# Gated cross attention and a grouped feed forward block on one core: the sums of token blocks are made ahead and kept in memory

## The reference

```python
x = x + jnp.tanh(g_xattn[0]) * xattn(_layernorm(x), ctx_2048, ctx_2048, wq, wk, wv, wo)
x = x + jnp.tanh(g_ffn[0]) * ffn(_layernorm(x), gate_w, mask_up_w, gate_proj_w, up_proj_w, down_proj_w, inv_map)

def xattn(x, k_cache, v_cache, wq, wk, wv, wo):
    q, k_new, v_new = (einsum('bsd,ed->bse', x, w) for w in (wq, wk, wv))
    k, v = concatenate([k_cache, k_new], 1), concatenate([v_cache, v_new], 1)
    attn = softmax(einsum('bqd,bkd->bqk', q, k) / sqrt(512))
    return einsum('bqd,ed->bqe', einsum('bqk,bkd->bqd', attn, v), wo)

def ffn(h, ...):
    scores = softmax(x @ gate_w.T)                       # 64 experts, the best 8 are kept as w_e
    flat = w_e[:, inv_map]                               # 8 groups of 8
    scalar = flat.sum(-1)
    soft = softmax(where(flat == 0, -1e9, flat))
    xg = x[:, None, :] + einsum('ngi,ghi->ngh', soft, mask_up_w)
    g, u = einsum('ngh,gih->ngi', xg, gate_proj_w), einsum('ngh,gih->ngi', xg, up_proj_w)
    return einsum('ng,ngh->nh', scalar, einsum('ngi,ghi->ngh', silu(g) * u, down_proj_w))
```

## Time and profile before

| | us |
|---|---|
| time before, three runs | 1113.67, 1112.12, 1113.27 (median 1113.27) |
| the profiled execution: its own time | 1115.06 |
| its span in the trace | 1113.3 |
| PE busy | 1061.3 (95%) |
| attention, until PE's last probability transposes (about) | 306 |
| quads 0 to 2, until product_1 of quad 3 | 404 |
| product_1 of quad 22, second pass | 732 |
| mean granted clock | 0.977 of full speed |

### The profile page before, as it was taken

The page is one execution under the profiler, slowest core; times in us unless marked ns, Lnnn a source line. Parts: engine busy times, 40 slices in busy tenths (PEclk is TensorE's granted clock), DMA queues, the critical chain, the costliest instruction groups (busy, mean ns, idle before and its releaser), DMA issues.

```text
span 1113.3 us, 14594 instructions
## 1 busy us (share of the span) xinstructions
PE 1061.3 (95%) x5388; PEld 903.4 (81%) x5388; DVE 754.8 (68%) x1328; ACT 378.4 (34%) x635; POOL 604.1 (54%) x479
## 2 busy tenths in 40 slices
PE   8999999999976779999999999979999999999997
PEld 7988998998865667887888888858888888888885
DVE  7775666666579648787787876776656665666554
ACT  5333333332332323433334332333233333332331
POOL 1212201210344656766687668767777777777751
PEclk9999999999988889999999999989999999999998
DMA  9112223323683411122212211472322112221202
GB/s 331 58 39 95 63 64 83 79 81 48 124 264 102 89 46 64 34 81 46 72 60 48 71 64 62 138 231 86 105 72 71 62 36 72 72 71 47 70 26 76
DMA packets 86861, 94.75 MB, mean 85 GB/s; under 512 B 20240, under 2 KB 71184, under 8 KB 86800
## 3 DMA queue, kind: packets, MB, share of 16 engines
q1 hardware_dynamic: 86432, 93.80, 28.8%
q10 hardware_dynamic: 368, 0.15, 0.0%
HBM read 70.67 MB, written 23.27 MB: 84 GB/s over the span
## 4 chain that ended last, share of the span: by engine, by line
PE 86%; DVE 7%; DMA 2%; issue 2%; POOL 1%; ACT 1%; SPq 1%; POOLq 0%; DVEq 0%; ACTq 0%
PE bank L67 42%; PE bank L1500 35%; PE bank L1506 3%; PE bank L1514 2%; PE bank L1331 1%; DMA x_raw<-x 1%; DMA soft_stacks<-soft_out 1%; DMA w_raw<-in_w_qkvo 1%; PE bank L1383 1%; DVE seed L906 0%; PE bank L1402 0%; POOL wd_lo L573 0%; SPq L426 0%; DVE soft L1026 0%; POOL wgu_lo L565 0%
## 5 line engine op out<-in xcount | busy, mean ns | idle before, releaser
L565 POOL TENSOR_TENSOR wgu_lo<-wgu_raw,wgu_hi 128x768 fp32r<-128x768 f32 (+1 forms) x132 | 214.6, 1633 | 97.7 <-ACT wgu_hi L756 95.5
L1500 PE MATMUL bank<-x2t_hi,wgu_lo 128*128 128x512 f32 x616 | 244.4, 397 | 17.8 <-ACT tmp L819 5.2
L1500 PE MATMUL bank<-x2t_lo,wgu_hi 128*128 128x512 f32 x616 | 242.5, 394 | 0.0
L1500 PE MATMUL bank<-x2t_hi,wgu_hi 128*128 128x512 f32 x616 | 242.1, 393 | 0.0
L756 ACT CAST wgu_hi<-wgu_raw 128x768 fp32r<-128x768 f32 (+1 forms) x132 | 95.7, 727 | 240.6 <-PE bank L1506 194.8
L1217 DVE TENSOR_TENSOR xres<-xres,bank 128x512 f32<-128x512 f32 x176 | 119.9, 682 | 63.2 <-PE bank L67 63.2
L1500 PEld LDWEIGHTS bank<-x2t_hi,wgu_lo 128*128 128x128 f32 x616 | 117.4, 191 | 44.7 <-issue 17.8
L67 PE MATMUL bank<-wd_hi,at_second 128*128 128x512 f32 x352 | 138.7, 394 | 0.0
L1500 PEld LDWEIGHTS bank<-x2t_hi,wgu_hi 128*128 128x128 f32 x616 | 117.2, 190 | 24.9
L1500 PEld LDWEIGHTS bank<-x2t_lo,wgu_hi 128*128 128x128 f32 x616 | 117.5, 191 | 23.4
L67 PE MATMUL bank<-wd_hi,at_first 128*128 128x512 f32 x264 | 105.4, 399 | 14.2 <-issue 13.0
(11 more groups left out here) (194 smaller groups left out, 2275.8 us busy)
## 6 DMA issues: line engine op xcount, KB each, us to landing
wgu_raw<-in_w_gate_up SPq DMA_DIRECT2D x44, 512.0 KB, 3.9
wd_raw<-in_w_down SPq DMA_DIRECT2D x22, 512.0 KB, 4.9
a_stacks<-a_stack SPq DMA_DIRECT2D x22, 192.0 KB, 1.8
a_stack<-a_stacks SPq DMA_DIRECT2D x22, 192.0 KB, 3.8
ctxt_raw<-in_ctx_t SPq DMA_DIRECT2D x8, 512.0 KB, 11.6
ctx_raw<-in_ctx SPq DMA_DIRECT2D x8, 512.0 KB, 9.3
x<-x_raw SPq DMA_DIRECT2D x8, 512.0 KB, 4.0
w_raw<-in_w_qkvo SPq DMA_DIRECT2D x6, 512.0 KB, 7.8
```

The source lines that it names most:

```text
L565: nc.gpsimd.tensor_tensor(wgu_lo[:, group], wgu_raw[quad.set][:, group], f32(wgu_hi[:, group]), ALU.subtract).then_inc(s_fw_lo, 1)
L1500: last = nc.tensor.matmul(out_bank[:], stationary, moving, start=begins and n == 0, stop=n == len(pairs) - 1, skip_group_check=True)
```

## The change

1. **Token sums in pieces.** The four sums are no longer made by DVE out of whole blocks. POOL makes them for 128 token columns at a time: SP's `load_piece` brings the two token chunks of x2 (512 rows of 128 columns each), `piece_sums` are four POOL subtractions of 128x256, ACT's `piece_high` casts 128x1024, POOL's `piece_low` subtracts 128x1024, and SP's `store_piece` writes both halves to two new tensors in memory, `token_sums_h` and `token_sums_l`. Pieces 0 to 3 (first pass) are made in attention iterations b = 5 and 6, two in each; pieces 4 to 7 (second pass) in quads 11 to 18.
2. **Blocks loaded ready made.** All seven token operands are loaded by `load_block(s, order)`, each with its own semaphore, in the order in which PE uses them. Those of the first pass start in iteration b = 7. Those of the second are a chain in quads 20 and 21: block 0 goes to a spare place, each further one to the home that the product before it in quad 21 has just read.
3. **PE's order at the transition.** Products 1 and 6 of quad 0 stand before `attend(B - 1)`, the rest of quads 0 and 1 is interleaved with the last batch's output projection, transposes and logits; products 1 and 6 of quad 1 stand before product 3 of quad 0. Quads 0 and 1 use other PSUM banks (`BANKS`). In quad 2 and in the last quad all four downs stand after product_3.
4. **Other orders.** ACT: group A of quad 0's weights before the `pt_hi` casts of b = 7, `act_high(quad, 0)` before the second silu, group B and C of quad 0 behind it; `weight_high` waits for the sums itself. POOL: `weight_sums` of the quad after next behind `weight_low` C. DVE: residual, norm and late rests of batches 6 and 7 moved in quads 0 and 1. SP: `load_soft` after the last outputs are in PSUM, `load_scalars` later still, `store_x2(B - 2)` in quad 0.
5. Several SBUF homes move (`wgu_hi`, `wgu_lo`, `tmp`, `soft_t`, `scalars`), and the loops with registers are written out.

```diff
+
+ORDER = (X00, T2, X10, T1, T3, T4, X11)
...
+            def load_piece(i):
+                first, second, _ = piece_tokens(i)
+                sp.wait_ge(s_piece_out, 32 * i)
+                sp.wait_ge(s_x2_raw_out, 16 * (second // S + 1))
+                for n, at in enumerate((first, second)):
+                    sp.dma_start(sums_raw[i // PIECES][:, n], x2_dram[:, :, at:at + PIECE]).then_inc(s_piece_in, 16)
+
+            def store_piece(i):
+                _, _, at = piece_tokens(i)
+                sp.wait_ge(s_piece_lo, i + 1)
+                for dram, part in ((th_dram, sums_hi), (tl_dram, sums_lo)):
+                    sp.dma_start(dram[:, :, :, at:at + PIECE].rearrange("p t k n -> p (t k) n"),
+                                 f32(part[i // PIECES][:]).rearrange("p c k n -> p (c k) n")).then_inc(s_piece_out, 16)
+
...
+                piece = 2 * (b - 5)
+                if b in (5, 6):
+                    if b == 5:
+                        sp.wait_ge(s_mu_lo, 1)
+                    load_piece(piece)
+                    store_piece(piece)
+                    load_piece(piece + 1)
+                if b == B - 1:
+                    sp.wait_ge(s_piece_out, 32 * PIECES)
+                    sp.wait_ge(s_q, 2 * B)
+                    load_block(0, 0)
+                    load_block(0, 1)
                 if b >= 2:
...
-                if b >= 3:
+                else:
+                    sp.wait_ge(s_k, 2 * B)
+                    load_block(0, 2)
+                    load_block(0, 3)
+                if b >= 3 and b + 1 < B:
                     store_soft(b - 3)
                 if b + 1 < B:
                     sp.wait_ge(s_vc_lo, b + 1)
                     sp.dma_start(ctx_raw[:], ctx_tiles[b + 1]).then_inc(s_ctx_in, 16)
+                if b in (5, 6):
+                    store_piece(piece + 1)
 
...
+            sp.wait_ge(s_v, NT)
+            for order in range(4, 7):
+                load_block(0, order)
+            sp.wait_ge(s_scores, NT)
+            load_weights(quads[1])
+            sp.wait_ge(s_o, NT)
             sp.wait_ge(s_soft_out, 16 * (B - 3))
+            for j in range(2):
+                load_soft(0, j)
...
-                if q == 1:
+                if q == 0:
                     store_x2(B - 2, x2r_hi, x2r_lo)
                 if q == 2:
...
+                if q in (11, 13, 15, 17):
+                    if q == 11:
+                        sp.wait_ge(s_flat, B)
+                    load_piece(PIECES + (q - 11) // 2)
+                if q in (12, 14, 16, 18):
+                    store_piece(PIECES + (q - 12) // 2)
...
+                    sp.wait_ge(s_piece_out, 32 * 2 * PIECES)
+                    load_block(1, 0)
...
+                    for order, read in enumerate((s_m1, s_m6, s_m2)):
+                        sp.wait_ge(read, q + 1)
+                        load_block(1, order + 1)
...
+                    for order, read in enumerate((s_m5, s_m7, s_m4)):
+                        sp.wait_ge(read, q + 1)
+                        load_block(1, order + 4)
...
+                pool.wait_ge(s_piece_in, 32 * (i + 1))
+                nc.gpsimd.tensor_tensor(chunk_0[:, low], chunk_1[:, low], chunk_0[:, low],
+                                        ALU.subtract).then_inc(s_piece_sum, 1)
+                pool.wait_ge(s_piece_sum, 4 * i + 1)
+                nc.gpsimd.tensor_tensor(chunk_1[:, low], chunk_1[:, high], chunk_1[:, low],
+                                        ALU.subtract).then_inc(s_piece_sum, 1)
+                pool.wait_ge(s_piece_sum, 4 * i + 2)
+                nc.gpsimd.tensor_tensor(chunk_1[:, high], chunk_1[:, high], chunk_0[:, low],
+                                        ALU.subtract).then_inc(s_piece_sum, 1)
+                pool.wait_ge(s_piece_sum, 4 * i + 3)
+                nc.gpsimd.tensor_tensor(chunk_0[:, high], chunk_0[:, high], chunk_1[:, high],
+                                        ALU.subtract).then_inc(s_piece_sum, 1)
+
+            def piece_low(i):
+                pool.wait_ge(s_piece_hi, i + 1)
...
+                if b in (5, 6):
+                    piece_sums(piece)
+                    piece_low(piece)
                 x2_whole(b - 2, ot_hi, ot_lo)
                 context_lo(b)
+                if b in (5, 6):
+                    piece_sums(piece + 1)
+                    piece_low(piece + 1)
 
             def weight_sums(quad):
                 raw = wgu_raw[quad.set]
...
-                        x2_whole(B - 2 + q, x2r_hi, x2r_lo)
-                    if q + 2 < QUADS:
-                        weight_sums(quads[q + 2])
+                    if q == 0:
+                        x2_whole(B - 2, x2r_hi, x2r_lo)
                     if q == 2:
                         for j in range(2):
                             wd_low(0, j)
                     weight_low(after, 2, GROUP_C)
-                if q + 1 < QUADS and quads[q + 1].begins_pass:
-                    sum_low(1, 3, T3)
-                    sum_low(1, 4, T4)
+                    if q + 2 < QUADS:
+                        weight_sums(quads[q + 2])
+                    if q in (11, 13, 15, 17):
+                        piece_sums(PIECES + (q - 11) // 2)
+                    if q in (12, 14, 16, 18):
+                        piece_low(PIECES + (q - 12) // 2)
...
+                if b in (5, 6):
+                    piece_high(2 * (b - 5))
                 eng.wait_ge(s_ctxt_in, 16 * (b + 1))
...
+                    add_down(below + n)
                 dve.wait_ge(s_m4, q + 1)
                 nc.vector.tensor_tensor(sums[:, SUM_1], sums[:, SUM_1], psum_b[:], ALU.add).then_inc(s_c21, 1)
                 dve.wait_ge(s_c21, q + 1)
...
+            quad, after = quads[0], quads[1]
+            product_1(quad)
+            product_6(quad)
+            attend(B - 1)
+            masked_products(quad)
+            product_2(quad)
+            product_5(quad)
+            pe.wait_ge(s_o_lo, NT)
+            pe.wait_ge(s_xn2, NT - 2)
+            transposes(xn, 4, s_x2)
+            product_7(quad)
+            for t in range(ST):
+                output(t, first=6)
+            soft_products(quad)
+            product_4(quad)
+            product_1(after)
+            product_6(after)
...
+            product_4(after)
+            product_3(after)
+            pe.wait_ge(s_x2_lo, NT)
+            logit_folds(7)
+            logits(B - 1, *late_tokens())
+
+            for quad in quads[2:]:
```

476 lines of the change are left out of this document (217 added, 259 removed).

## The result

The changed kernel takes 1134.26 us (median of four runs, 1131.28 to 1140.45) where the kernel before takes 1113.47 beside it: ratio 1.0189, 95% interval 1.0167 to 1.0211. It is slower by 1.9 per cent; the prediction had 1110.0, faster, with a range from 1090 to 1125. The profiled execution took 1133.18, its span is 1131.4, 18.1 more than before.

The account below looks back on a forecast made before the run. The prediction took PE, busy 95% of the span, as the bound. Its terms, -24.9 - 9.3 + 22.2 + 7.2 + 1.5 = -3.3 us, gave 1111.8 for the profiled execution and 1110.0 for the median, range 1090 to 1125.

Parts of the forecast that it names:

- D: Quads 11 to 18: piece sums on POOL delay the downs, PE waits 1.8 in four quads; +7.2 us, range 1 to 14.
- E: The rest: product_4 waiting in the last quad and act_high before the second silu; +1.5 us.
- B: Pass boundary: nothing computed there any more, only 7 MB loaded; -9.3 us, range -6.5 to -10.3.
- A: Transition from attention's end to quad 3: lost PE time won back despite a new 4.9 stall; -24.9 us, range -18 to -41.
- C: Attention iterations 5 and 6: x2 stores wait on SP behind landed piece stores, stalling PE; +22.2 us, range 17.4 to 29.6.
- R1: Rival: the cost in iterations 5 and 6 is hidden, 0 to 11 us, giving 1088 to 1099; chance 0.22.
- R2: Rival: POOL bounds quads 11 to 18, costing 21 us, giving 1124; sign: quads 12 to 18 over 19 us; chance 0.16.

Follow-up runs that it names:

- e2: Changed kernel without pieces 4 to 7; the second pass loads the first pass's token sums: 1119.71 us, ratio 1.0051.
- e14: Changed kernel with the store of the routing scalars in iteration 7 moved behind the weights of quad 1: 1142.91 us, ratio 1.0240.
- e15: e14 without DVE's wait for the scalar store in iteration 7: 1127.81 us, ratio 1.0116.
- e4: Changed kernel with the second pass's scalar rows loaded behind the last three token blocks in quad 21: 1131.07 us, ratio 1.0120.
- e8: Changed kernel with, in iterations 5 and 6, x2 stores ahead of the first piece's store and its ACT cast behind the query casts: 1127.52 us.
- e16: e11 with first-pass pieces spread over iterations 5 to 7, scalar store behind quad 1's weights, no DVE wait for it in iteration 7: 1087.88 us, ratio 0.9776.
- e5: Changed kernel with the second pass's piece sums and rests moved into POOL's idle time ahead of group C: 1123.46 us, ratio 1.0082.
- e11: e9 with e10's edit added: 1103.02 us, ratio 0.9893.
- e10: Changed kernel with ACT's act_high(quad, 0) back behind the second silu: 1131.02 us, ratio 1.0133.
- e3: Changed kernel with POOL's weight sums back ahead of the low part of group C: 1131.98 us, ratio 1.0146.
- e7: e2 with the weight sums ahead of group C again from quad 3 on: 1122.28 us, ratio 1.0050.
- e9: Changed kernel with the edits of e8, e5 and e4, and weight sums ahead of group C in quads 3 to 11 and from 20: 1109.43 us.

## Why the prediction was wrong

The forecast, -3.3, was a sum of terms with both signs; measured, it is +18.2. The step that failed is D: what the second pass's pieces cost in quads 11 to 18 was put at 7.2 and is 15.6 by e2, and with that alone set right the forecast would have been slower than before. D is 8.4 of the 21.5 us, E 7.2, B 5.4 and A 4.1, and C gives 3.6 back.

- **A, the transition** (-24.9, range -18 to -41): measured -20.8; -22.2 from iteration 7's transposes on, and iteration 7 itself 1.4 longer, which no term had. The chain came as told up to quad 2: less the 18.6 us of the iterations, product_1 of quad 0 starts at 313.2 and quad 2 at 357.6, for 313.3 and 357.6. The miss is in quad 2, 7.04 of stall where 3 to 4 were allowed. The 4.9 for the new stall (measured 4.52) was luck: its cause was given as the four block transfers ahead of the weights, while e14 and e15 show it to be the scalar store, though that was in the prediction's own rows.
- **B, the pass boundary** (-9.3, range -6.5 to -10.3): measured -3.9, outside. "Only 7 MB loaded" left out the scalar rows' transfers in the middle of the queue (four of them; the expectation of e4 says eight, which is both halves), 4.2 us by e4. The range's upper end does not follow from its own "0 to 3" either: 10.3 less 3 is 7.3.
- **C, iterations 5 and 6** (+22.2, range 17.4 to 29.6): measured +18.6. The mechanism, x2 stores behind a landed piece store, is real but only 8 of it; most of the other 10 are POOL's piece beside DVE's short steps. That the range held is luck in good part. R1, that it is hidden, was wrong for the kernel as changed, and right for iteration 5 of e8 and both iterations of e16.
- **D, the pieces in quads 11 to 18** (+7.2, range 1 to 14): measured +19.8 over quads 11 to 21, of which e2 gives the pieces 15.6 and leaves 4.2 to E. The mechanism in the even quads was right, a wait of about 2 us at the first down for 1.8, but the term took no slow clock behind it and put the odd quads at nothing. The even quads lost 11.1 for 7.2, and quad 13 lost 4.0, by POOL's rest beside DVE's short operations and the clock. The stretch came near R2's 21, but the time is 10 above R2's 1124, and quads 15 and 17 stay under its 19 us. R2's reading, that no idle time of POOL is usable, is not right: e5 put the same work into idle time and got 13 us back.
- **E, the rest** (+1.5): measured 3.0 in quads 3 to 10, 1.5 in quads 23 to 42, and the 4.2 that e2 left in quads 11 to 21. The 3.0 go when `act_high` stands behind the second silu and the weight sums ahead of C (e11); neither edit alone does it (e10; e3, e7, e9). The 4.2 and the 1.5 remain open.

The prediction took the slow clock to come after stalls of 3.8 us or more. In these traces it also came after 3.16, 2.23 and 1.86 us, and in the kernel before after the 1.44 at 306.25. Against the median the sum had one more error: four terms that may each be off by several us, with a forecast of their small difference, made a range that ended at 1125.

## What to carry to other kernels

An engine's average idle time does not say what added work costs: the same eight pieces cost 34 us (18.6 and 15.6) in the changed kernel and at most 5 in e16, by what they were queued ahead of on POOL, ACT and SP. For each inserted instruction ask what stands behind it on its engine, which of that PE waits for, and whether a neighbour's short operations run at the same time. A wait that is moved with a transfer (as in e14) has to be looked for on the other engines too.

## What the runs showed of the hardware

- Short TENSOR_TENSOR and TENSOR_SCALAR operations of DVE that start while a POOL operation runs end with it in these rows: 2.05, 2.06 and 1.91 us instead of 0.2 to 0.3, with ends 0.04 to 0.15 us apart. In e8 `var_eps` took 2.37 from 233.25, beside a POOL operation of 2.40 from 233.19. TENSOR_REDUCE and RECIPROCAL were not held (0.27 and 0.25), and neither was `kt_lo` in e8, which reads PSUM: 0.69 from 250.33, beside a POOL operation of 2.35 from 249.88.
- Stalls of nearly the same length lowered the granted clock or did not: 2.23 us in quad 12 and 2.19 in quad 14, with 0.92 and 1.00 over the quad. Quad 8 of the changed kernel took 19.82 us in one profile (stall 2.29, clock 1.00) and 21.39 in the other (2.21, 0.92). So one profile's stage of quads can be 1.6 us off another's with the same kernel.
- A store of 8 KB in 4 byte pieces holds back what is queued behind it: 29 GB/s moved from 310 to 315 us, 298 in the same window once it stood elsewhere, and one SP issue of 8.75 us.
- The piece stores, in runs of 512 bytes, land in 3.6 and 5.3 us (median), close to the x2 stores' 3.7 and 4.8 in the same kernel:

```profile
token_sums_h<-sums_hi SPq DMA_DIRECT2D x8, 512.0 KB, 3.6
token_sums_l<-sums_lo SPq DMA_DIRECT2D x8, 512.0 KB, 5.3
...
x2h<-ot_hi SPq DMA_DIRECT2D x6, 512.0 KB, 3.7
x2l<-ot_lo SPq DMA_DIRECT2D x6, 512.0 KB, 4.8
```

By the Trainium skill ("DMA: Bandwidth & Descriptors", Specifications) runs of 512 bytes just suffice for the full rate, which the prediction weighed. These times agree with it; no run moves the same data in shorter runs. That C came near the low end (17.4) that went with it is luck, since half of C had another cause.
